# A graph layer with a mixture of experts on one core: filling the bins at the front is dropped, and the last body computes one more late batch

## The reference, cut to what matters

```python
N, D, E = 8192, 128, 8                     # tokens (graph nodes), model width, experts
def layer(x, adj, ...):
    h = relu(adj @ layernorm(x) @ gcn_w + gcn_b)        # adj is dense, 8192 x 8192 f32
    h = layernorm(h) * ln_g + ln_b
    xz = h @ w_in                                       # 128 -> 2*256
    u = silu(causal_conv4(xz[:, :256]) + conv_b);  z = xz[:, 256:]
    dt, B, C = softplus(...), ..., ...                  # from u @ w_xp
    for t in range(N):                                  # the scan: 256 channels, 16 states
        s = exp(dt[t] * A) * s + dt[t] * B[t] * u[t];   y[t] = s @ C[t] + u[t] * D_skip
    x = x + (y * silu(z)) @ w_out
    v = layernorm(x)                                    # feed-forward, one of 8 experts a token
    H = gelu(v @ W1 + b1)                               # 128 -> 512
    p = softmax(H @ Wg + bg);  e = argmax(p)
    return x + p[e] * (H @ Wd[e] + bd[e])               # 512 -> 128
```

## Time and profile before

| | |
|---|---|
| median of 3 runs | 1708.79 us (1708.24 to 1717.01) |
| the profiled execution's own time | 1713.96 us |
| its span (first to last instruction) | 1712.2 us |
| VectorE busy | 1516.5 us, 89% |
| TensorE busy | 1426.8 us, 83%; mean granted clock 0.926 |
| ScalarE, GpSimd busy | 904.2 us, 791.5 us |
| DMA | 476.91 MB, mean 279 GB/s |

### The profile page before, as it was taken

The page is one execution under the profiler, slowest core; times in us unless marked ns, Lnnn a source line. Parts: engine busy times, 40 slices in busy tenths (PEclk is TensorE's granted clock), DMA queues, the critical chain, the costliest instruction groups (busy, mean ns, idle before and its releaser), DMA issues. The chain is left out here.

```text
span 1712.2 us, 16034 instructions
## 1 busy us (share of the span) xinstructions
PE 1426.8 (83%) x4115; PEld 668.0 (39%) x4115; DVE 1516.5 (89%) x1931; ACT 904.2 (53%) x1580; POOL 791.5 (46%) x395
## 2 busy tenths in 40 slices
PE   5998888888879998998898989989989894535478
PEld 2433333333334444443343434444444442123244
DVE  8057979999999999999999999999999999998843
ACT  3043536373536647383837465564748384655531
POOL 0013334444544455554555555555555555457532
PEclk9999999999999999999999999999999997676689
DMA  8878989999999898898898898988988885423440
GB/s 311 282 260 311 329 325 338 337 343 382 352 351 314 307 319 300 293 313 281 296 316 296 290 313 287 318 286 303 317 300 305 287 299 190 154 99 137 154 131 15
DMA packets 157805, 476.91 MB, mean 279 GB/s; under 512 B 19693, under 2 KB 41760, under 8 KB 157586
## 3 DMA queue, kind: packets, MB, share of 16 engines
q1 hardware_dynamic: 114098, 324.56, 53.9%
q10 hardware_dynamic: 38560, 139.48, 23.7%
q0 software_dynamic: 5056, 11.87, 1.8%
HBM read 445.75 MB, written 32.97 MB: 280 GB/s over the span
## 5 line engine op out<-in xcount | busy, mean ns | idle before, releaser
L1215 PE MATMUL ps_adj<-ring,nodes 128*128 128x512 f32 x2048 | 962.7, 618 | 108.7 <-DMA ring<-adj 58.3
L503 POOL TENSOR_TENSOR h_c<-hidden,bc_ring 128x1024 f32<-128x1024 f32 x256 | 602.2, 2352 | 841.4 <-DVE inject L1087 641.8
L1004 DVE TENSOR_TENSOR_SCAN hidden<-decay,state,inject 128x512 f32<-128x512 f32 x512 | 627.4, 1267 | 36.4 <-ACT decay L590 13.4
L1215 PEld LDWEIGHTS ps_adj<-ring,nodes 128*128 128x128 f32 x2048 | 393.1, 197 | 625.6 <-issue 458.3
L590 ACT ACTIVATE decay<-dt_sb,negA 128x512 f32<-128x512 f32 x512 | 340.2, 713 | 31.9 <-issue 18.4
L1087 DVE TENSOR_TENSOR inject<-dtu_sb,bc_ring 128x1024 f32<-128x1024 f32 x256 | 314.0, 1227 | 7.1 <-DMA bc_ring<-bc_dram 6.2
L1047 DVE TENSOR_TENSOR y_sum<-y_sum,h_c 128x1024 f32<-128x1024 f32 x224 | 273.6, 1221 | 9.8 <-POOL h_c L503 6.7
L583 ACT COPY state<-hidden 128x2 f32<-128x2 f32 x255 | 49.0, 192 | 415.9 <-DVE hidden L1004 415.3
L480 POOL DMA_INDIRECT out<-o_sb,out_at x68 | 101.5, 1492 | 65.9 <-DVE o_sb L905 51.6
L475 POOL DMA_INDIRECT bins<-rec,dest x60 | 86.8, 1447 | 10.3 <-issue 9.7
L1141 PE MATMUL ps_e<-wd_ring,H 128*128 128x128 f32 x448 | 61.3, 293 | 9.5 <-ACT H L726 9.5
(11 more groups left out here) (202 smaller groups left out, 1273.0 us busy)
## 6 DMA issues: line engine op xcount, KB each, us to landing
ring<-adj SPq DMA_DIRECT2D x512, 512.0 KB, 5.9
bc_ring<-bc_dram ACTq DMA_DIRECT2D x256, 512.0 KB, 6.1
wd_ring<-wd_rows SPq DMA_DIRECT2D x64, 288.0 KB, 3.4
bins<-nodes SPq DMA_DIRECT2D x32, 516.0 KB, 8.5
got<-bins SPq DMA_DIRECT2D x60, 129.0 KB, 3.5
nodes<-x_rows ACTq DMA_DIRECT2D x8, 512.0 KB, 12.1
x_tile<-x_rows SPq DMA_DIRECT2D x16, 256.0 KB, 7.3
wd_rows<-Wd SPq DMA_DIRECT2D x8, 256.0 KB, 8.0
```

Source lines behind the costliest of these rows:

```text
L503: nc.gpsimd.tensor_tensor(h_c[:, s % 2], hidden[:, s % 2], over_halves(bc_ring[:, s % BC_RING, 1]), ALU.mult).then_inc(hc_ready, 1)
L1004: scan = nc.vector.tensor_tensor_scan(hidden[:, s % 2, h], decay[:, s % 2, h], inject[:, h], state[:, h, s:s + 1], ALU.mult, ALU.add)
L1215: last = nc.tensor.matmul(ps_adj[:, 0], nodes[:, m], ring[:, g % RING, m % GROUP], start=(m == 0), stop=(m == J - 1))
```

## The change

1. `clear_bins` goes. In its place one DMA of 1,032 KB fills the first 1,024 rows of the bins, in body 1, slot 0 (`fill_first_blocks`). In the last body, once the ends of the bins are known, SP writes 128 rows behind each of the 8 tails (`fill_behind_tails`). VectorE makes their places with two small instructions (`tail_at`). `control` works with the head's sign turned, with as many instructions as before, and one more runs at the start.
2. For bodies up to 4 `residual_product` moves on PE from the end of slot 2's list to the beginning of slot 1's.
3. In body 0 the first two front steps move from slot 6 to slot 7, and one adjacency group with them.
4. The last body: GpSimd's four scatters of slot 1 are split over slots 1 and 2, those of slots 6 and 7 are put before `h_c`, its writes of results move by a slot; the twelfth batch finishes in slot 9 instead of 10; columns(0), the Gelus of f = 0 and 1 and finish_late(0) come a slot or more earlier; choose(2) comes in slot 11; PE gets expert(1), columns(2) and the hidden units of f = 2 in slot 12, in front of the last `residual_product`.
5. Behind the last body three late batches' experts are left instead of four, and two batches' transposes and hidden units instead of three.

The diff, cut to its core:

```diff
-        0: (0, 0, 0, 0, 0, 0, 1, 2, 2, 2, 3, 2, 2, 3, 3, 3),
+        0: (0, 0, 0, 0, 0, 0, 0, 3, 2, 2, 3, 2, 2, 3, 3, 3),
         1: (0, 0, 0, 2, 2, 2, 2, 2, 2, 2, 2, 2, 2, 2, 2, 2),
         2: (0, 0, 2, 2, 2, 2, 2, 2, 2, 2, 2, 2, 2, 2, 2, 2),
         3: (0, 3, 2, 2, 2, 2, 2, 2, 2, 2, 2, 2, 2, 2, 2, 3)}
 LEAD = {0: (4, 3, 3, 3, 3, 3), 1: (4, 3, 2), 2: (3, 3), 3: (4,)}
-FRONT = {0: (6, 6, 7, 7, 8, 8, 9, 10, 11, 12, 12, 13, 14, 15, 15, 15),
+FRONT = {0: (7, 7, 7, 7, 8, 8, 9, 10, 11, 12, 12, 13, 14, 15, 15, 15),
          1: (2, 2, 3, 3, 4, 5, 6, 7, 8, 9, 10, 11, 12, 13, 14, 15),
          2: (2, 2, 3, 3, 4, 5, 6, 7, 8, 9, 10, 11, 12, 13, 14, 15),
          3: (1, 1, 2, 3, 4, 5, 6, 7, 8, 9, 10, 11, 12, 13, 14, 15)}
@@ -59,7 +59,6 @@
     BLOCKS = T // P
...
-        zero_in = [sem(f"zero_in{n}") for n in range(AREAS)]
...
+            def fill_first_blocks():
+
+                sp.dma_start(bins.ap()[0:EXPERTS * P].rearrange("(p n) c -> p (n c)", p=P),
+                             nodes[:].rearrange("p j d -> p (j d)")[:, 0:EXPERTS * REC]).then_inc(zero_in, 16)
+
+            def fill_behind_tails():
+
+                sp.wait_ge(tail_step, 2)
+                for e in range(EXPERTS):
+                    first = sp.value_load(tail_at[0:1, e:e + 1], min_val=0, max_val=SPACE - 1)
+                    sp.dma_start(bins.ap()[bass.ds(first, P, EXPERTS)], spare).then_inc(swept, 16)
...
-                    if i in (1, 2, 3):
-                        k = SLOTS * (i - 1) + s
-                        for n in range(AREAS * PARTS * k // (3 * SLOTS), AREAS * PARTS * (k + 1) // (3 * SLOTS)):
-                            clear_bins(n)
+                    if i == 1 and s == 0:
+                        fill_first_blocks()
...
                     if s == 13 and i == TILES - 1:
+                        fill_behind_tails()
                         c.wait(scat_in, -1, 16 * BLOCKS)
+                        sp.wait_ge(swept, 16 * EXPERTS)
                         late_rows(0)
-                        late_experts(0, -2)
-                    if s == 14 and i == TILES - 1:
                         c.wait(o_ready, -4, PICKS + 1)
                         late_rows(1)
+                        late_experts(0, -2)
                         late_experts(1, -2)
+                        late_rows(2)
+                        late_experts(2, None)
...
-            late_rows(2)
-            late_experts(2, None)
...
-                out_slots = (0, 2, 3, 4) if fast else OUT_SLOTS
+                out_slots = (0, 3, 4, 5) if fast else OUT_SLOTS
...
+                    if fast and s in (6, 7):
+                        c.wait(dest_step, -1, 5)
+                        c.wait(xn_ready, -1, BLOCKS)
+                        c.wait(id_step, -1, 1)
+                        for b in (2 * s - 12, 2 * s - 11):
+                            scatter_rows(q, b)
...
-                    if scatter and s in ((1,) if fast else (1, 2, 3, 4)):
-                        for b in range(BLOCKS) if fast else (s - 1,):
+                    if scatter and s in ((1, 2) if fast else (1, 2, 3, 4)):
+                        for b in (2 * s - 2, 2 * s - 1) if fast else (s - 1,):
                             scatter_rows(p, b)
-                    if fast and s == 6:
-                        c.wait(dest_step, -1, 5)
-                        c.wait(xn_ready, -1, BLOCKS)
-                        c.wait(id_step, -1, 1)
-                    if fast and s in (6, 7):
-                        for b in (2 * s - 12, 2 * s - 11):
-                            scatter_rows(q, b)
-                    if fast and s in (11, 12):
+                    if fast and s in (10, 11):
                         c.wait(o_ready, -4, PICKS + 1)
-                        for j in (2 * s - 22, 2 * s - 21):
+                        for j in (2 * s - 20, 2 * s - 19):
                             scatter_out(p, j)
...
+                    if fast and s == 9:
+                        columns(0)
                     if fast and s == 10:
-                        columns(0)
-                    if fast and s == 11:
                         gelu(0, (0, 1))
                         act.preload_act_table_set(EXP_LN_SET)
-                    if fast and s == 12:
+                    if fast and s == 11:
                         columns(1)
                         gelu(0, (2, 3))
                         act.preload_act_table_set(EXP_LN_SET)
-                    if fast and s == 13:
-                        gelu(1, (0, 1))
+                    if fast and s in (12, 13):
+                        gelu(1, (0, 1) if s == 12 else (2, 3))
                         act.preload_act_table_set(EXP_LN_SET)
                     if fast and s == 15:
-                        gelu(1, (2, 3))
+                        columns(2)
+                        gelu(2, (0, 1))
+                        gelu(2, (2, 3))
...
-            columns(2)
-            gelu(2, (0, 1))
+            columns(3)
+            gelu(3, (0, 1))
             logit_columns(c, False)
-            gelu(2, (2, 3))
+            gelu(3, (2, 3))
             c.wait(gate_step, -1, 2)
             nc.scalar.activation(expo[:], logit[:], ACT.Exp).then_inc(expo_ready, 1)
             act.wait_ge(coef_t_done, 1)
             nc.scalar.copy(coef_t[:], ps_y[0:BLOCKS * EXPERTS, 0, 0:P]).then_inc(coef_t_ready, 1)
-            for f in (3, 4):
-                columns(f)
-                gelu(f, (0, 1))
-                gelu(f, (2, 3))
+            columns(4)
+            gelu(4, (0, 1))
+            gelu(4, (2, 3))
...
-                nc.vector.tensor_tensor(cand[:], over_picks(head[:]), offset[:], ALU.add).then_inc(mark, 1)
+                least = float(BASE + EXPERTS * (1 if flush else P))
+                nc.vector.tensor_tensor(cand[:], over_picks(head[:]), offset[:], ALU.subtract).then_inc(mark, 1)
                 after(1)
-                nc.vector.scalar_tensor_tensor(out=has[:], in0=cand[:], scalar=float(EXPERTS * (1 if flush else P)),
-                                               in1=over_picks(tail[:]), op0=ALU.add, op1=ALU.is_le
-                                               ).then_inc(mark, 1)
+                nc.vector.tensor_tensor(has[:], cand[:], over_picks(tail[:]), ALU.add).then_inc(mark, 1)
                 after(2)
-                nc.vector.scalar_tensor_tensor(out=key[:], in0=has[:], scalar=float(BASE), in1=cand[:],
-                                               op0=ALU.mult, op1=ALU.subtract).then_inc(mark, 1)
+                nc.vector.scalar_tensor_tensor(out=key[:], in0=has[:], scalar=least, in1=cand[:],
+                                               op0=ALU.is_ge, op1=ALU.mult).then_inc(mark, 1)
...
                         destinations(c, -1)
+                        c.wait(dest_step, -1, 5)
+                        nc.vector.tensor_copy(tail_at[:], tail[:]).then_inc(tail_step, 1)
                         c.wait(ctrl_step, -4, 10)
+                        dve.wait_ge(tail_step, 1)
+                        nc.vector.tensor_scalar(tail_at[:], tail_at[:], SPACE - 1, None, ALU.bitwise_and
+                                                ).then_inc(tail_step, 1)
                         choose(0)
                     if fast and s == 8:
                         choose(1)
-                    if fast and s == 14:
+                    if fast and s == 13:
                         finish_late(0)
-                    if batch and s == (10 if fast else 15):
+                    if fast and s == 11:
+                        choose(2)
+                    if batch and s == (9 if fast else 15):
                         c.landed(row_in, -4, p)
                         finish(c, -4, p, got[:, p], ps_e[:, 1])
...
             gated(c, 1)
-            choose(2)
+            finish_late(1)
             residual(c, 1)
+            choose(3)
             norm_shift(c)
-            finish_late(1)
-            choose(3)
+            finish_late(2)
             choose(4)
             logits_below_max(c)
             probability(c, 1)
             c.wait(gate_step, -1, 7)
             nc.vector.tensor_tensor(coef[:], pick_bf[:], over_experts(prob_col[:, 1]), ALU.mult).then_inc(coef_ready, 1)
-            finish_late(2)
+            finish_late(3)
             dve.wait_ge(base_done, 1)
             nc.vector.tensor_tensor(sums, ps_y[:, 0].rearrange("p (b c) -> p b c", b=BLOCKS), x1_rows[:, 1], ALU.add
                                     ).then_inc(sum_step, 1)
             for u in range(5):
                 combine(u)
-            finish_late(3)
-            combine(5)
-            combine(6)
             finish_late(4)
-            combine(7)
+            for u in range(5, 8):
+                combine(u)
...
+                    if ffn and s == 1 and i <= 4:
+                        c.wait(y_ready, -1, 1)
+                        c.wait(dest_step, -1, 0)
+                        residual_product()
...
-                    if ffn and s == 2:
```

(27 more changed lines are left out.)

38 lines of the change are left out of this document (17 added, 21 removed).

## The result

The changed kernel takes 1692.03 us (median of 4 runs, 1687.21 to 1696.46), the kernel before 1708.99 us on the same chip (4 runs, 1708.24 to 1717.01). The ratio is 0.9889, 95% interval 0.9866 to 0.9913: faster by 17.0 us. The forecast was 1692.8 us and a gain of 16. Measured twice more, against the kernel before on the same chip, the gain is 22.1 and 20.9 us, so the time fitted better than the sum behind it.

A forecast was written before the change was run, and what follows sets the result against it. VectorE was taken as the bound between about 600 and 1500 us, with waits at the front and in the last body. Last body and end -9 and front -7.0 made -16: 1708.8 to 1692.8 us, range 1685 to 1702.5.

The forecast's parts named there:

- Behind the last body: Chain over PE after the last body: one batch fewer saves 8.0 us and a pause of about 0.6, sum -8.6.
- The last store: At the very end: the last unit's sum and last store were to stay behind the last product as before.
- The last body up to the gate: VectorE up to its last gate: added 2.9 and 0.4, removed 1.9 for GpSimd and 3.0 for decays, sum -1.6 us.
- PE in the last body: Late batches' loads, experts and hidden products ahead of the last residual product, which starts 0.5 us later but takes 1.95.
- At norm_shift: Behind the last gate: residual product ends 1.3 us sooner, choose(3) in between adds 1.0; net -0.3.
- The front: Bodies 0 to 4: +0.6, 0, -1.2, -2.2 and -4.2 us in turn, sum -7.0.
- The +1.6 for the fill in slot 0: Body 1: 1,032 KB of filling instead of 516 KB ahead of tile 2's last adjacency groups, +1.6 us at 338 GB/s.
- Body 0's +0.6: Body 0: PE does all three groups first, not two of them in the shadow of ScalarE's steps, +0.6 us.
- three signs of being wrong: Residual waits for PE by more than 3 us, late_rows(0) starts no sooner, or body 4's waits stay.
- only the end pays: Rival: front waits only change their name in bodies 1 to 4; gain 9 less 0.6, 1700.4 us; chance 0.17.
- PE's new list delays the residual: Rival: lower clock and late landing leave the end a gain of 1 or 2, front 7; 1700.5 us; chance 0.13.
- body 1 pays too: Rival: tile 2 arrives earlier or ScalarE's chain is shorter, up to 10 us more gain; 1683 us; chance 0.12.

The follow-up runs named there:

- after: The changed kernel itself in its first profiled execution, which took 1687.21 us; its runs had a median of 1692.03 us.
- a: The changed kernel measured again, unaltered: 1692.42 us, ratio 0.9881 to the kernel before.
- j: The changed kernel measured a third time, unaltered: 1690.18 us, ratio 0.9869 to the kernel before.
- b: The changed kernel with clear_bins, residual_product's old slot 2 and body 0 put back, so only last body and end stay changed: 1700.89 us, ratio 0.9919.
- i: The changed kernel with the 32 clearing writes back in bodies 1 to 3 and without fill_behind_tails, its wait and tail_at: 1698.07 us, ratio 0.9939.
- z_before: The kernel before, unchanged, profiled and measured once more: 1710.20 us over 8 executions, ratio 0.9992.
- e: The changed kernel with body 0 as before, two front steps and one adjacency group back in slot 6: 1689.09 us, ratio 0.9862.
- f_late_fill: The changed kernel with the 1,032 KB fill issued in slot 8 of body 1 instead of slot 0: 1692.87 us, ratio 0.9893.
- g: The changed kernel with expert(1), columns(2) and the hidden products of f = 2 on PE behind the last residual_product: 1700.28 us, ratio 0.9933.
- k: The changed kernel with body 0 as before, measured a second time beside the changed kernel on one chip: 1690.39 us, ratio 0.9871.
- d: The changed kernel with residual_product back in slot 2 for all bodies, the clearing writes still gone: 1697.06 us, ratio 0.9906.

## Why the prediction came out as it did

**Behind the last body: right.** From the start of the first unit to the end of the last it was 49.68 us, now 40.90: -8.8 against -8.6.

**The last store: a missed term of -1.4.** The prediction said that "the last unit's sum and the last store stay behind the last product as before". From the end of the last vector instruction to that of the span it was 4.2 us in both executions of before, 2.8 in after, a, j and b. Before, the last thing was not the plain store but the last batch's four indirect writes on GpSimd, as the chain of the kernel before says:

```profile
1703.28 0.87 DVE o_sb L905 x3
...
1706.22 0.98 POOL out L480
...
1708.79 0.98 POOL out L480
```

Now the last expert stands two units earlier and these writes are out at 1677.5. The prediction followed PE back from the last unit and didn't read the last rows of the chain.

**The last body up to the gate: right in its sum.** The terms were -1.9 for GpSimd, -3.0 for decays, +3.3 for the new instructions: -1.6. Waits at L1050 fell from 6.0 to 3.5 (-2.5), for decays from 4.1 to 1.6 (-2.5). Gate to gate, 101.5 and 99.7 before against a mean of 98.8 in eleven executions with the new last body (all but i): -1.8. The decays are the loose part: 2.0 instead of 4.1 in z_before and 0 to 1.7 in the changed kernels.

**PE in the last body: right.** Counted against the last gate, late_rows(0) was forecast 47.7 us ahead and started 46.5 ahead. expert(0) was forecast 25.7 ahead and came 25.6 ahead; expert(1) 9.7 and 9.8; the residual product 3.4 behind and 2.3 behind, at 1.95 us as forecast. The eight writes took 8.8 us of issue (8 forecast), held the rows up by 1.4 to 2.4 and cost nothing. Their landing, which no row had shown, is in the trace of after, as count, KB each and median us to landing:

```profile
bins<-nodes SPq DMA_DIRECT2D x8, 129.0 KB, 3.3
```

The Trainium skill (DMA: Bandwidth & Descriptors, section Anatomy of one DMA) puts the fixed time of a DMA at about 2 us, fitted on GpSimd's path; with its rate for the size that makes some 2.3 us, an estimate. The 3.3 us here are longer, so the trace doesn't bear the page's figure out for these writes, which SyncE issues.

One step was right in its time and wrong in its wait. The prediction had expert(0) wait for its weights, behind late_rows(1). By the trace's landing records these had landed at 1587.9. What let it start at 1588.98 was ScalarE's Gelu, as its row says and as the row of the kernel before already said (1611.93, [3.25 <-ACT nodes L761]). In the lists of PE and ScalarE the transposes of f = 1's rows stand in front, at 1585.06 once these rows had landed, then the copy, a table load and the Gelu. Rows and weights are issued one right behind the other, so the count of eight issues and a landing came out at the right time partly by luck.

**At norm_shift: mis-sized by 1.3.** Forecast was norm_shift 0.3 sooner with a gate 1.6 sooner, so 1.3 more between the two. It was 9.0 us before and 9.0 after (9.0 to 10.3 in the experiments). The residual product came 1.1 us sooner than counted, for expert(1) took 5.85 and not 7. From there to the first unit 1.1 us were lost again in after (16.6 against 15.4). PE idled 2.71 us ahead of the transposes, before 1.48, and from their start to that of the seventh product behind them it took 6.9 us instead of 5.7. In j and e that stretch was 15.2 us, no longer than before, but there norm_shift came 0.3 to 0.4 later behind the gate.

**The front: right in body 4, right about the place in body 1, too small in body 3.** The prediction said for body 1 that the wait moves to ScalarE's chain and is worth 0 within wide bounds. In all ten executions with the residual product early, norm_shift comes 11.12 or 11.13 us behind the copy of tile 2's adjacency product, in the four with it late 12.90 or 12.91: the chain lost 1.79 us, about the residual product's own time, and so did the stretch from the copy to the next gate. When tile 2 arrives varies by 4.8 us between executions of the very same kernel (227.5 to 232.3 us), and that sets body 1. The +1.6 for the fill in slot 0 can't be seen: f_late_fill has no sooner copy (228.98). Bodies 1 and 2 together were forecast at -1.2; the mean of before, z_before and b is 192.2 us, of the six with the whole front change or all but body 0 (after, a, j, g, e, k) 190.8: -1.4. Body 3 was forecast at -2.2 and gives -3.3 (94.2 to 90.9). Body 4 was forecast at -4.2 and gives -4.0 (96.8 to 92.9). But the sum for body 3 had only the wait for the residual product in it, which was to go by the move. d, with that product in its old place, has body 3 at 91.5 and a wait of 0.9 instead of 2.2, so the relief of DMA pays most of it. Body 0's +0.6 can't be told from its spread. The front is 8.5 us by the medians of b and a and 8.7 by these bodies, against 7.

**The sum.** -1.4 for bodies 1 and 2, -3.3, -4.0, -1.8 for the last body and -8.7 behind it (79.8 to 71.1, a mean of ten, without g and i) make -19.2 us. The ratios of three measurements, 0.9889, 0.9881 and 0.9869, make -19 to -22 on 1711. By the stretches the forecast of -16 was short by some 3 us: 1.4 the store, 1.1 body 3, 0.6 the cost of body 0 that was counted and can't be seen, the rest two or three tenths here and there. What the residual product gained against the count was lost again ahead of the first unit. The forecast hit the time to 0.8 us partly by luck, since the median of before from which it was counted, 1708.8, was itself the lowest of the four that were measured (1714.5, 1711.4, 1711.1).

**The signs.** No wait for ps_y at L941 in bodies 1 to 4, 8.95 us before the front's product in body 0, the residual product at 1.95 us and 41 us for the units came as said. The 7 to 10 us for ScalarE in body 1 were 5.9 in after (1.1 and 4.8), 5.6 in a_again and 10.6 in j_again: 4.8 at norm_shift each time, and the scan's wait for a decay as late as tile 2 is. None of the three signs of being wrong came: VectorE waited 1.9 us for the residual, late_rows(0) started 46.5 us ahead of the gate instead of 43.4, and body 4's waits are gone.

**The rivals.** That only the end pays falls with b, d and the bodies 3 and 4. That PE's new list delays the residual falls with g. That body 1 pays too is open in its size: the 1.8 us of the chain are shown, an earlier arrival of tile 2 from less filling is not. The mean of the copies is 231.2 us in the five with the full filling (227.7 to 233.4), 229.6 in the nine without (227.5 to 232.3). From the copy of tile 1 to that of tile 2 it is 76.5 and 76.3 us, so less filling doesn't bring tile 2 sooner by anything that these traces can tell.

**Left open.** Why tile 2 arrives early in one execution and late in the next. The copy of tile 0 is at 75.2 to 77.6 us in all, so most of the difference comes up behind it, while PE waits for the groups of the adjacency and DMA moves less. Why DMA is slower there in one execution was not tried. How much the move of the residual product is worth by itself is also open, between the some 2 us of the bodies and the 4.6 of the medians.

## What to carry to other kernels

An operation moved forward on an in-order engine pays only if the engine isn't late there for another reason: in bodies 3 and 4 the move alone brought nothing and the relief of DMA alone nearly all. Read in the row itself what released an instruction, before counting the wait that one expects there. Follow the last chain to its last row, stores included, before saying that the end stays as it is. And before two traces are subtracted, look at how far each profiled execution lies from its own median; here 10 of 27 us were that.

## What the hardware showed that was not expected

An idle TensorE in front of a short product cost more than work that delayed it. After 14.9 us of idling (g_behind), and after 9.6 us in the kernel before, 16 matmuls took 3.78 us at a granted clock of 0.50; behind other work they took 1.95 us at 1.00. Delaying them by 1 us with useful work ended them 0.8 us sooner.

The chain from the copy of tile 2's adjacency product to norm_shift, over ScalarE, PE and VectorE, had the same length to 0.01 us in ten executions on several chips (11.12 or 11.13), while its start varied by up to 6 us with the adjacency that DMA delivers (227.5 to 233.4). Bodies 5 to 14 together take 932.2 to 932.6 us in all fourteen. Between the three profiled executions of the changed kernel the front, where PE waits for DMA, makes 5.6 us, the last body 1.0 and the end 1.3. None of them was one of the long executions near 1696 us, so where those lose their time is not shown.
